# A fused gated cross-attention and FFN block: key rows packed as 64 of two heads to a tile, with column halves and quarters on TensorE

## The reference

```python
x = x + tanh(g_xattn) * xattn(layernorm(x), ctx, ctx)
x = x + tanh(g_ffn)   * ffn(layernorm(x))

def xattn(q, k, v):                       # H = 8 heads of D = 128
    f_q, f_k, f_v = proj(q), proj(k), proj(v)     # layernorm, then @ w_in.T
    dots = einsum('hqnd,hqmd->hqnm', f_q, f_k)
    cosine = dots / (norm(f_q) x norm(f_k))
    var = q_ratio x k_ratio               # outer product, ratios from the rows' variances
    mixed = cw * cosine + vw * cosine * decorr_scale + ww * var    # weights per head
    out = einsum('hqnm,hqmd->hqnd', mixed, f_v)
    return concat_heads(out) @ w_out.T + b_out

def ffn(x):                               # 16 heads of 16
    softmax attention on x @ Wq, x @ Wk, x @ Wv; z @ Wo; l2norm; @ Wff; l2norm; gelu
```

## Time and profile before

| | us |
|---|---|
| median of 3 runs | 1376.34 (1375.95 to 1377.22) |
| the profiled execution | 1375.92 |
| its span | 1373.3 |
| TensorE (PE) busy | 1268.7, 92% |
| VectorE (DVE) busy | 1117.0, 81% |
| ScalarE (ACT) busy | 1027.6, 75% |
| GpSimd (POOL) busy | 191.5, 14% |
| mean granted TensorE clock | 0.977 |

### The profile page before, as it was taken

The page is one execution under the profiler, slowest core; times in us unless marked ns, Lnnn a source line. Parts: engine busy times, 40 slices in busy tenths (PEclk is TensorE's granted clock), DMA queues, the critical chain, the costliest instruction groups (busy, mean ns, idle before and its releaser), DMA issues.

```text
span 1373.3 us, 34972 instructions
## 1 busy us (share of the span) xinstructions
PE 1268.7 (92%) x10770; PEld 797.6 (58%) x10770; DVE 1117.0 (81%) x3164; ACT 1027.6 (75%) x3398; POOL 191.5 (14%) x130
## 2 busy tenths in 40 slices
PE   4999887999999999999999999999999999999864
PEld 2667565656656565656575656565656565665521
DVE  6986665897979797979797979798989889797853
ACT  5666232687878787979696979787888878787876
POOL 2352120102020202020101101010101020202000
PEclk9999899999999999999999999999999999999976
DMA  8440011606151424242424233342415050605140
GB/s 252 140 151 19 12 33 41 199 11 193 29 176 45 161 61 153 68 153 69 153 69 141 80 122 99 100 122 78 144 59 162 31 185 6 202 19 173 35 154 16
DMA packets 163127, 141.25 MB, mean 103 GB/s; under 512 B 9326, under 2 KB 150799, under 8 KB 163088
## 3 DMA queue, kind: packets, MB, share of 16 engines
q1 hardware_dynamic: 163088, 140.76, 32.9%
HBM read 87.00 MB, written 42.55 MB: 94 GB/s over the span
## 4 chain that ended last, share of the span: by engine, by line
PE 59%; DVE 13%; issue 11%; ACT 2%; DMA 1%; SPq 1%; POOL 1%; DVEq 0%; POOLq 0%; ACTq 0%; PEldq 0%
PE work L893 17%; PE work L895 15%; PE work L894 15%; PE attended L1391 7%; PE score L1380 4%; DVE nm L1672 2%; PE work L1283 2%; DVE Vpl L1569 2%; DVE l2s L1641 1%; DVE Gl L1581 1%; DMA sqE<-sq_rows 1%; ACT prob L1479 1%; DVE x2S L1635 1%; DVE qst L1594 1%; SPq L1220 1%
## 5 line engine op out<-in xcount | busy, mean ns | idle before, releaser
L1479 ACT ACTIVATE prob<-score,nm 128x256 f32<-128x256 f32 x1024 | 470.9, 479 | 25.6 <-DVE nm L1672 19.3
L1672 DVE TENSOR_REDUCE nm<-score 128x2 f32<-128x512 f32 x512 | 337.1, 680 | 14.1 <-PE score L1380 13.3
L1479 ACT ACTIVATION_READ_ACCUMULATOR prob<-score,nm 128x1 f32 x1024 | 218.3, 213 | 0.0
L1594 DVE BATCH_NORM_STATS2 qst<-work 128x6 f32<-128x128 f32 x512 | 113.6, 283 | 102.9 <-PE work L895 102.9
L1391 PE MATMUL attended<-prob,vsp 128*32 128x256 f32 x2048 | 138.6, 395 | 14.2 <-DVE vsp L1687 11.9
L1380 PE MATMUL score<-qstack,kstack 64*128 64x256 f16 x1024 | 102.3, 279 | 17.2 <-ACT prob L1479 16.3
L893 PE MATMUL work<-woutTh,fvph 128*128 128x256 f16 x384 | 105.4, 274 | 5.6 <-DVE Vpl L1569 4.6
L1526 POOL TENSOR_TENSOR rq<-qft,mhalf 128x32 f32<-128x32 f32 x16 | 86.8, 5426 | 164.6 <-DVEq L1601 164.6
L894 PE MATMUL work<-woutTl,fvph 128*128 128x256 f16 x384 | 104.7, 273 | 0.0
L895 PE MATMUL work<-woutTh,fvpl 128*128 128x256 f16 x384 | 104.7, 273 | 0.0
L893 PE MATMUL work<-wTh,xTh 128*128 128x512 f16 x256 | 97.9, 382 | 1.9 <-DVE fvpl L1581 1.9
(11 more groups left out here) (327 smaller groups left out, 3272.4 us busy)
## 6 DMA issues: line engine op xcount, KB each, us to landing
qstack<-parts SPq DMA_DIRECT2D x64, 256.0 KB, 3.8
kstack<-parts SPq DMA_DIRECT2D x64, 256.0 KB, 4.2
sqE<-sq_rows SPq DMA_DIRECT2D x64, 154.0 KB
s_xin<-in_x SPq DMA_DIRECT2D x8, 1024.0 KB, 6.1
xin<-in_x SPq DMA_DIRECT2D x16, 512.0 KB, 3.7
x2S<-in_x SPq DMA_DIRECT2D x16, 512.0 KB, 8.0
parts<-qh SPq DMA_DIRECT2D x32, 256.0 KB, 2.4
parts<-ql SPq DMA_DIRECT2D x32, 256.0 KB, 2.5
```

Source lines behind the costliest of these rows:

```text
L1479: nc.scalar.activation(prob[:, g % PG, e, j + jj, :], sc[n % SC][:, jj * NQ:(jj + 1) * NQ], ACT.Exp, bias=nm[:, u + jj:u + jj + 1], accum_ ...
L1594: last = nc.vector.bn_stats(qst[:, t, 4 * half + h, :], bank(e)[:, h * DH:(h + 1) * DH])
L1672: nc.vector.tensor_reduce(nm[:, u:u + 2], sc[n % SC][:, :].rearrange("p (u q) -> p u q", q=NQ), AX.X, ALU.max, negate=True).then_inc(max_r ...
```

## The change

1. Packing. Tiles 0 to 3 now hold the first or last 64 of the 77 keys of two heads each (an even head in rows 0 to 63, an odd one in rows 64 to 127). The 13 left over of all eight heads stand in the fifth tile, 16 rows each. `fvp` has blocks of 96 columns, `G` of 80, with zeros behind the 77 keys.
2. V writes a 64-row half of the bank for each head, 3 products of 64 columns; the fifth tile is written in 32-row quarters, each by an even and an odd head whose windows leave the other's 16 rows zero.
3. d uses the same tiles: a 64-column product for each half, a 32-column one for each quarter. All tiles have 128 rows.
4. The correction rows (query ratios, bias) leave the fifth tile. They stand in tiles of their own, mE and vE (73 rows: high at 0, low at 32, a second high at 64), and y has one more product for each row block. ScalarE and VectorE write mE directly, so `wqT` and the step `wq` are gone.
5. G has eight chunks of two heads.
6. sqE is loaded by five DMAs in two steps, sqe0 and sqe1; `ldr` has three.
7. ORDER is another one, with 49 bank chunks in place of 47.

```diff
 ORDER = """
-rk V0 qs1 V1 V0.h V0.l S0 qpow V1.h G0 M0 G1 G0.h V1.l S1 X0 M1 G2 G1.h G0.l X1 G1.l a1 M2 G2.h S2 a1.h V2 G2.l X2
-a1.l G3 qs2 V2.h wq M3 a0 G3.h V2.l a0.v M4 V3 X3 aux M5 ldx G3.l X4 ldr R0 S3 V4 V3.h M6 X5 M7 V3.l sqe X6 S4 V5 M8
...
-X28 S15 pk1 q1.o pk0.h M30 X29 pq0 pk0.l X30 R6 M31 pq1 pk1.h L2 X31 pk1.l P6 pq0.h R7 pq1.h pq0.l P7 pq1.l O1 parts0
-parts1 E3 L3 O2 O1. O3 O2. q2 O3. back0 back1 q3 F1 q2.o pv0 q3.o F2 q4 pv0.v q5 q4.o F3 q6 q5.o q7 q6.o back2 back3
-pv1 q7.o F4 pv1.v out res
+rk S0 S1 M0 V0 M1 V1 X0 qs1 V0.h V1.h X1 V0.l a1 qpow M2 a1.h G0 V1.l G0.h X2 a1.l G1 S2 M3 G1.h V2 G0.l X3 G1.l G2 M4
+G4 V2.h S3 M5 G2.h G4.h V2.l X4 qs2 G2.l a0 G4.l X5 G3 R0 V3 M6 a0.v S4 M7 G3.h G5 aux V3.h P0 G3.l ldy M8 G5.h ldx X6
+V3.l G6 G6.h G5.l V4 X7 M9 V5 G6.l sqe0 V4.h R1 S5 G7 X8 M10 P1 V4.l G7.h V5.h G7.l fk0 X9 V5.l z S6 fk0.h d0 sqe1 X10
+M11 fk0.l X11 fk1 ldr M12 d0.o S7 fk1.h d1 M13 E0 X12 R2 fk1.l d2 m0.h L0 d3 X13 M14 m0.l X14 d1.o P2 d2.o m1.h M15 d4
+m2.h m1.l X15 m2.l d5 d3.o d4.o S8 m3.h S9 zT0 M16 m4.h y0 m3.l zT0.h M17 X16 d5.o M18 X17 R3 m5.h M19 X18 m4.l S10
+zT1 X19 m5.l P3 M20 zT0.f M21 S11 zT1.h R4 y1 M22 E1 zT0.l L1 zT1.f y0.o X20 M23 zT1.l X21 O0 y1.o X22 ln1 S12 P4 X23
+O0. S13 M24 fk2 lpow M25 q0 fk2.h ln2 X24 X25 fk2.l zz0 q0.o zz1 zz0.h S14 M26 zz1.h q1 R5 X26 zz0.l P5 zz1.l M27 pq0
+M28 X27 q1.o pk0 E2 X28 M29 R6 S15 pq0.h pq1 M30 X29 pq0.l X30 M31 pk1 L2 X31 P6 pk0.h R7 pk1.h pk0.l P7 pq1.h parts0
+pq1.l O1 E3 L3 pk1.l O2 O1. O3 O2. q2 O3. back0 q3 F1 q2.o parts1 pv0 q3.o F2 q4 pv0.v q5 q4.o F3 q6 q5.o back3 q7
+q6.o pv1 q7.o F4 pv1.v res back1 out back2
 """.split()
+def value_block(h, b2):
+    return FS * (2 * h + b2) + LEFT * (h % 2)
+def left_block(h, b2):
+    return FS * (2 * h + b2) + (64 if h % 2 == 0 else -16)
+    def key_tile(t, b2):
+        if t == HT - 1:
+            return [(32 * j, 32, GS * (4 * j + 2 * b2) + 64) for j in range(H // 2)]
+        return [(64 * odd, 64, GS * (4 * t + 2 * b2 + odd) + LEFT * odd) for odd in range(2)]
 # V on TensorE
-                        heads = tile_heads(t)
-                        for h in heads:
-                            last = products(nc, bk[:, n * DIM:(n + 1) * DIM],
-                                            fvp, (ALL, slice(window(t, h, b2), window(t, h, b2) + P)),
-                                            w["woutT"], (ALL, h), h == heads[0], h == heads[-1])
+                        if t < HT - 1:
+                            for m, (x, y) in enumerate(("hh", "hl", "lh")):
+                                for h in (2 * t, 2 * t + 1):
+                                    at = value_block(h, b2)
+                                    last = nc.tensor.matmul(bk[64 * (h % 2):64 * (h % 2) + 64, cols], fvp[x][:, at:at + 64],
+                                                            w["woutT"][y][:, h, :], start=m == 0, stop=m == 2)
+                            continue
+                        for odd in range(2):
+                            for m, (x, y) in enumerate(("hh", "hl", "lh")):
+                                for j in range(H // 2):
+                                    at = left_block(2 * j + odd, b2)
+                                    last = nc.tensor.matmul(bk[32 * j:32 * j + 32, cols], fvp[x][:, at:at + 32],
+                                                            w["woutT"][y][:, 2 * j + odd, :], start=odd == 0 and m == 0,
+                                                            stop=odd == 1 and m == 2)
 # d on TensorE
+                            for m, (x, y) in enumerate(("hh", "hl", "lh")):
+                                for row, size, at in key_tile(t, b2):
+                                    last = nc.tensor.matmul(bk[row:row + size, n * 2 * P:(n + 1) * 2 * P], G[x][:, k, at:at + size],
+                                                            xT[y][:, k, b2 * NQ:(b2 + 1) * NQ], start=k == 0 and m == 0,
+                                                            stop=k == KT - 1 and m == 2)
 # y on TensorE, after the five tiles
+                        last = nc.tensor.matmul(bk[:, r * DIM:(r + 1) * DIM],
+                                                mE[0:Y_ROWS, c * NQ + r * P:c * NQ + (r + 1) * P], vE[0:Y_ROWS, c, :],
+                                                start=False, stop=True)
 # a1.h on ScalarE
-                    nc.scalar.activation(wqT["h"][:], bank(e)[0:H, :], ACT.Copy, scale=MS).then_inc(hi_ready[lead(e)], 1)
+                    wait_filled(act, a - 1, "y1")
+                    nc.scalar.activation(mE[0:H, :], bank(e)[0:H, :], ACT.Copy, scale=MS)
+                    nc.scalar.activation(mE[LL_ROW:LL_ROW + H, :], bank(e)[0:H, :], ACT.Copy, scale=MS).then_inc(hi_ready[lead(e)], 1)
 # SP
+                elif step == "sqe0":
+                    for t in (0, 1):
+                        sp.dma_start(sqE[:, t, :], bc(sq_rows[2 * t:2 * t + 2, :].unsqueeze(1), [2, 64, PR])).then_inc(sq_in[0], 16)
+                elif step == "sqe1":
+                    for t in (2, 3):
+                        sp.dma_start(sqE[:, t, :], bc(sq_rows[2 * t:2 * t + 2, :].unsqueeze(1), [2, 64, PR])).then_inc(sq_in[1], 16)
+                    sp.dma_start(sqE[:, HT - 1, :], bc(sq_rows[:, :].unsqueeze(1), [H, 16, PR])).then_inc(sq_in[1], 16)
```

More of the change, by code:

```diff
@@ L41 @@
 HM_TILES = [(0, 1), (2, 3), (4,)]
[L42 to L45, removed]
 SB = NB // NG
@@ L996, in half @@
     return group, e, 2 * i, 2 * (4 * group + 2 * e + i)
[L999 to L1008, removed]
+def value_block(h, b2):
+    return FS * (2 * h + b2) + LEFT * (h % 2)
+def left_block(h, b2):
+    return FS * (2 * h + b2) + (64 if h % 2 == 0 else -16)
+SQ_LOADS = [2, 3]
 def main_phase(nc, ctx, w, x_rows, out_rows, rk_rows, kr_rows, sq_rows, fixed_rows, parts):
@@ L1030, in main_phase @@
     rk_all, rkc = sb("rk_all", [P, HT, NB]), sb("rkc", [P, HT, 2])
-    aux, sqT, wqT = sb("aux", [P, 2, PT, H]), sb("sqT", [H, PR]), pair("wqT", [H, PR])
+    aux, sqT = sb("aux", [P, 2, PT, H]), sb("sqT", [H, PR])
     st4, qst, qft = sb("st4", [P, PT, 2]), sb("qst", [P, PT, H, 6]), sb("qft", [P, 5, PT, H])
@@ L1109, in emptied @@
             b2, tiles = c // 3, HM_TILES[c % 3]
-            r, n = HM_ROWS[tiles[0]], len(tiles)
-            return (mT[half][0:r, b2, tiles[0]:tiles[-1] + 1, :],
-                    md[0:r, c % 2, 0:n * 2 * P].rearrange("p (t n) -> p t n", n=2 * P), MS)
+            n = len(tiles)
+            return (mT[half][:, b2, tiles[0]:tiles[-1] + 1, :],
+                    md[:, c % 2, 0:n * 2 * P].rearrange("p (t n) -> p t n", n=2 * P), MS)
         bk = bank(e)
@@ L1298, in a_part @@
                 elif kind == "G":
-                    k, (lo_h, hi_h) = c // 3, HEAD_PARTS[c % 3]
-                    wait_drained(pe, a, f"fk{c % 3}")
-                    rows = bk[:, 0:(hi_h - lo_h) * PM].rearrange("p (b h m) -> p b h m", b=2, m=MK)
-                    for h in range(lo_h, hi_h):
+                    k, j = c // 4, c % 4
+                    wait_drained(pe, a, f"fk{(2 * j + 1) // 3}")
+                    rows = bk[:, 0:2 * PM].rearrange("p (b h m) -> p b h m", b=2, m=MK)
+                    for h in range(2 * j, 2 * j + 2):
                         keys = {half: key_cols(half, h, h + 1) for half in "hl"}
-                        last = products(nc, rows[:, :, h - lo_h, :], w["wN"], (ALL, h, slice(k * P, (k + 1) * P)), keys, (ALL,))
+                        last = products(nc, rows[:, :, h - 2 * j, :], w["wN"], (ALL, h, slice(k * P, (k + 1) * P)), keys, (ALL,))
                 elif kind == "V":
@@ L1509, in _ @@
         def _(pool):
+            nc.gpsimd.memset(md[0:NB, 1, 0:P], 0.0).then_inc(init, 1)
+            nc.gpsimd.memset(mE[:], 0.0).then_inc(init, 1)
+            nc.gpsimd.memset(vE[:].rearrange("p b o -> p (b o)"), 0.0).then_inc(init, 1)
             pool.wait_ge(xT_ready, KT)
             for half in "hl":
-                nc.gpsimd.memset(fvp[half][:, 0:2 * H * PAD].rearrange("p (n c) -> p n c", c=PAD)[:, :, 0:127], 0.0)
-                nc.gpsimd.memset(fvp[half][:, 2 * H * PAD:PADW], 0.0).then_inc(init, 1)
+                nc.gpsimd.memset(fvp[half][:].rearrange("p (n c) -> p n c", c=FS)[:, :, MK:FS], 0.0).then_inc(init, 1)
+            for half in "hl":
+                for k in range(KT):
+                    nc.gpsimd.memset(G[half][:, k, :].rearrange("p (n c) -> p n c", c=GS)[:, :, MK:GS], 0.0).then_inc(init, 1)
             nc.gpsimd.memset(vsp[:], 0.0).then_inc(init, 1)
```

99 lines of the change are left out of this document (45 added, 54 removed).

## The result

The changed kernel takes 1671.87 us (median of 4 runs, 1667.77 to 1677.70), beside 1376.14 for the kernel before on the same chip: 1.2154 times as long, 95% interval 1.2114 to 1.2193. I had forecast 1358. It is 296 us slower, and outside the range.

The account below looks back on a forecast made before the run. TensorE was taken to set the pace, VectorE 0.35 us behind in the first stretch. TensorE's -2.8 us a turn gives 1.2: 14 x 1.2 = 16.8, plus 1.5 for turn 1; 1375.92 - 18.3 = 1357.6, median 1358, range 1349 to 1371.

Parts of the forecast that it names:

- SP's queue: SP's loads: two wq loads go, 12 sqE loads (4.26 us of issue) become five; fewer issues were given nothing.
- E: Rival: stack load back1 comes late for S4, 3 us margin gone by 3 us, 1400; 0.08 with other order slips.
- G in eight chunks: Emptying G's chunks: +0.3 us on VectorE and +0.4 on ScalarE a turn, TensorE's 48 products the same.
- This costs nothing while VectorE has work.: Head of the turn: TensorE waits 1.5 to 3 us at a1 for aux, at no cost.
- 52.4 busy in the first stretch, VectorE is now the last.: Before the turn's tail: TensorE 52.4 us busy, VectorE 54.5; of TensorE's 2.8 saved, the turn gains 1.2.
- Rival B: Whole turn: VectorE keeps 2.1 us idle, ScalarE's added 1.0 delays its exponentials; 1373 to 1378 us, chance 0.14.
- a1. ... nothing is added.: ScalarE writes a1's high part twice, +0.6 us on ScalarE; nothing added through VectorE's a1.l, which waits for it.
- the slots: V and d products on TensorE: two halves or four quarters share one 0.109 us slot; V gains 3.92 us.
- C: Rival: pairs of column products in V and d cost more than a slot; 1408 at 0.160 us, chance 0.08.
- D: Rival: quarter products of V and d limited by issue, 0.22 us a slot; 1373 us, chance 0.04.
- signs of being wrong: Half pair over 0.12 us, a turn below 69.4 or above 71 us, or TensorE waiting on kstack.
- 0.69 faster: Whole kernel: summed chance of a time more than 0.2%, 2.8 us, below the kernel before.

Follow-up runs that it names:

- e1: The changed kernel with tiles 0 to 3 of sqE loaded by eight DMAs of 64 rows in place of four two-row-source loads: 1411.88 us (ratio 1.0268).
- e3: The changed kernel with only tiles 0 and 1 of sqE loaded by four DMAs of 64 rows, tiles 2 and 3 as they were: 1539.84 us (1.1188).
- e8: The kernel before the change with only G in eight chunks of two heads in place of six: 1405.22 us (1.0203).
- e14: e1 with G in six chunks again, keeping the order of the change: 1413.50 us (1.0256).
- e9: e1 with 20 more products, their result overwritten, issued by TensorE ahead of its wait for aux in a1: 1406.18 us (1.0217).
- e18: e13 without ScalarE's second copy of a1; SP copies those 8 rows by DMA: 1396.39 us (1.0151).
- e17: e16 without ScalarE's second copy of a1; SP copies those 8 rows by DMA: 1387.82 us (1.0085).
- e16: e13 with V's column-half products in tiles 0 to 3 issued twice: 1396.10 us (1.0136).
- e13: e1 with G in six chunks again and the order of the kernel before: 1399.93 us (1.0165).
- e7: e1 with V's column-half products in tiles 0 to 3 issued twice: 1492.66 us (1.0838).

## Why the prediction was wrong

**The failed step is "SP's queue".** I wrote that the 12 sqE loads "become five", that "the bytes are as before", and "I give the fewer issues nothing". I counted issues and bytes, and not how a transfer is spread. Four of the five loads move 50 GB/s, where the loads of before ran in 225, and that is 260 of the 296 us (e1, e3). The sum had no term for it and none of the rivals named it; E came nearest, a late load, but it was another load. The rule of the Trainium skill, DMA: Bandwidth & Descriptors, Why a DMA increments its semaphore by 16 and not by 1, would have made it one: 4 x 256 KB on 2 of 16 engines.

**The step that fell second is "G in eight chunks".** Its terms, 0.3 and 0.4 us, count what a drain takes. e8 measured 2.0 us a turn in the kernel before: the term left out is what TensorE waits for banks. The price depends on the order of the chunks (e14), and the forecast priced the two apart.

**"This costs nothing while VectorE has work."** The wait of `a1` came as predicted, 2.5 us in the turn above for 1.5 to 3. But the clock fell to half behind it, and TensorE was busy for 6.02 of the next 6.44 us (the changed kernel's window; 0.50 is the clock):

```profile
730.56:737.00 6.44, 6.02 (x55) 3.95 (x56) 5.93 (x13) 5.86 (x20) 4.07 (x1) 0.50 0.73 200
```

e9 prices that at 6 us in all, with an interval that touches e1's.

**"52.4 busy in the first stretch, VectorE is now the last."** The wait held: TensorE had slack, VectorE and ScalarE were nearly full. The gain did not. Of TensorE's 2.8 us I took 1.2 as gain. e18 against e17, with 2.6 us of V taken off, shows a loss of 0.84 a turn (877.02 against 866.97 over twelve). Where VectorE and ScalarE are full, the work taken off TensorE became idle time, and behind it the clock was lower. Rival B (no gain) was nearest to the truth here.

**"a1. ... nothing is added."** ScalarE's second copy, 0.59 us, costs 0.44 us a turn with V twice (e16 72.69, e17 72.25) and 0.27 with V once (e13, e18). `mE` on VectorE waited for it, 0.5 us a turn in e16, and ScalarE has little slack in the head of the turn.

**Right were** the slots: halves and quarters side by side at 0.11 us, so rivals C and D are out. E, the late stack load, didn't come about: in the full turns of the changed kernel TensorE never waits for kstack. Of the signs of being wrong that I had named, the turn showed it: 90.3 us, above 71. A slip without weight: the parts listed for "0.69 faster" add up to 0.71.

## What to carry to other kernels

When a change merges transfers, write down for each the slowest dimension of source and target and how many DMA engines it can use, before comparing issues and bytes; a broadcast with a short leading dimension is the case to look for, and a DMA share that stands at 2/16 in a window, as here, shows it. Work taken off TensorE was worth nothing here, where the engines that empty its banks are full, and even cost 8.6 us, with the clock lower behind the idle time. Ask how full *they* are, and count drains and banks as well as products. Test a supposed saving by adding it back: if doubling the products doesn't slow the kernel, they weren't worth removing.

## What the runs showed of the hardware

- With source [2, 64, 512] the loads ran at a DMA share of 0.13, two of 16 engines: 50 GB/s, 5.2 us for 256 KB. Loaded by 64 rows each, the window over them has 242 GB/s. SP was held for 4.75 us on average by the two issues behind the first two, and 5.15 by the fifth.
- 20 products whose result is thrown away, in a wait of 2.46 us, kept the granted clock at 1.00 (0.97 without) and made a turn 0.6 us shorter (e9; the medians' intervals touch).
- Column quarters with fp16 and 256 columns run four to a slot of 0.11 us, 0.027 each; halves two to a slot. The step from halves to quarters cost 0.10 us more (743.13).
- e7's loop fetched instructions anew (106 packets in 12 turns, none in e1's) and TensorE stood still for 4.0 us a turn; e16, with more matmuls, has 25 packets in all.
